# Attention masks written by ScalarE into the score bank, layer-norm spreading by transposes, and the second FFN block in another PSUM bank

## The reference

```
qkv = shift(x) @ Wqkv                    # 16 heads of 64
q, k = rotary(l2norm(q) * qs), rotary(l2norm(k) * ks)
sim  = q @ k^T * 8                       # windows of 32 queries, 64 keys (own window and the one before)
sim  = where(key > query or key < query - 32 or no such key, -max, sim)
x    = softmax(sim) @ v @ Wo + x
h    = layernorm(shift(x)) * g + b
a, gate = split(h @ W1 + b1)             # 341 + 341 columns
x    = (a * gelu(gate)) @ W2 + b2 + x
```

## Time and profile before

| | |
|---|---|
| time, median of 3 runs | 2706.54 us (2702.59 to 2709.49) |
| the profiled execution's own time | 2708.14 us |
| its span, first to last instruction | 2706.4 us |
| PE / DVE / ACT / POOL busy | 91% / 62% / 58% / 59% |
| PE weight loads busy | 62% |
| mean granted clock of TensorE | 0.964 of 2.4 GHz |
| first and last mask product (L558) | 198.6 and 2044.4 us |

### The profile page before, as it was taken

The page is one execution under the profiler, slowest core; times in us unless marked ns, Lnnn a source line. Parts: engine busy times, 40 slices in busy tenths (PEclk is TensorE's granted clock), DMA queues, the critical chain, the costliest instruction groups (busy, mean ns, idle before and its releaser), DMA issues.

```text
span 2706.4 us, 57956 instructions
## 1 busy us (share of the span) xinstructions
PE 2462.3 (91%) x23054; PEld 1687.6 (62%) x23054; DVE 1677.8 (62%) x2517; ACT 1581.8 (58%) x3162; POOL 1607.0 (59%) x931
## 2 busy tenths in 40 slices
PE   5769999999999999999999999999997888889998
PEld 3435666666666666666666666666664666656665
DVE  2347667666766666666666666766672888852222
ACT  1126666666666676667666666666662566643333
POOL 1039777777777777777777777777771322211111
PEclk8769999999999999999999999999997899989999
DMA  4002223222232222322233222322223000000000
GB/s 103 0 20 60 53 52 72 64 62 50 57 75 64 55 53 61 74 65 53 53 74 72 52 52 52 80 64 55 50 55 104 1 1 1 1 1 1 5 5 8
DMA packets 77196, 127.13 MB, mean 47 GB/s; under 512 B 24948, under 2 KB 48770, under 8 KB 76930
## 3 DMA queue, kind: packets, MB, share of 16 engines
q1 hardware_dynamic: 76930, 123.42, 19.6%
HBM read 26.56 MB, written 1.07 MB: 10 GB/s over the span
## 4 chain that ended last, share of the span: by engine, by line
PE 49%; DVE 20%; ACT 16%; issue 12%; POOL 3%; SPq 0%; DMA 0%; POOLq 0%; ACTq 0%; DVEq 0%
PE bank L601 6%; PE bank L526 6%; DVE qk L1200 6%; ACT qk L891 5%; PE bank L804 4%; PE bank L613 4%; PE bank L563 4%; PE obank L583 3%; ACT vp L903 3%; PE obank L814 2%; PE bank L814 2%; DVE n L1207 2%; PE bank L738 2%; PE lnbank L547 2%; ACT aoT L936 2%
## 5 line engine op out<-in xcount | busy, mean ns | idle before, releaser
L1200 DVE TENSOR_TENSOR qk<-bank,tab 128x1024 f32<-128x1024 f32 x384 | 470.3, 1225 | 438.2 <-ACT qk L891 438.2
L1497 POOL TENSOR_TENSOR qk<-qk 128x1024 f32<-128x1024 f32 x192 | 454.0, 2365 | 362.3 <-DVE qk L1200 362.2
L1501 POOL TENSOR_TENSOR rn<-n2m,cst 128x16 f32<-128x16 f32 x192 | 562.9, 2932 | 16.0
L526 PE MATMUL bank<-wqk,xs 128*128 128x512 f32 x768 | 400.5, 603 | 6.2 <-issue 3.7
L1505 POOL TENSOR_TENSOR qk<-qk,rn 128x1024 f32<-128x1024 f32 x192 | 365.4, 1903 | 28.1 <-POOL rn L1501 0.9
L891 ACT ACTIVATE qk<-bank 128x512 f32<-128x512 f32 x384 | 228.7, 596 | 173.2 <-PE bank L526 165.2
L537 PEld LDWEIGHTS bank<-cst,qk 128*128 128x128 f32 x1536 | 192.4, 141 | 209.8 <-issue 197.4
L1509 POOL TENSOR_TENSOR lnr<-lnv,cst 128x2 f32<-128x2 f32 (+1 forms) x88 | 66.4, 755 | 404.1 <-DVE lnv L1094 404.1
L924 ACT ACTIVATE px<-sh 128x512 f32<-128x512 f32 x192 | 121.4, 632 | 256.2 <-DVE sh L1216 255.6
L537 PE MATMUL bank<-cst,qk 128*128 128x128 f32 x1536 | 231.7, 274 | 6.6 <-POOL qk L1505 6.6
L1207 DVE TENSOR_REDUCE n<-qk 128x16 f32<-128x1024 f32 x192 | 232.2, 1209 | 0.0
(11 more groups left out here) (194 smaller groups left out, 4429.1 us busy)
## 6 DMA issues: line engine op xcount, KB each, us to landing
vp<-vp SPq DMA_DIRECT2D x672, 130.0 KB, 2.4
wqk<-in_L_ffn_Wqkv SPq DMA_DIRECT2D x24, 256.0 KB, 3.1
wv<-in_L_ffn_Wqkv SPq DMA_DIRECT2D x6, 512.0 KB, 3.6
wo<-in_L_ffn_Wo SPq DMA_DIRECT2D x6, 512.0 KB, 4.3
xs<-Z SPq DMA_DIRECT2D x48, 64.0 KB, 2.4
xs<-Z SPq DMA_DIRECT2D x48, 63.8 KB, 2.3
kT<-rel_by_distance SPq DMA_DIRECT2D x1, 2048.0 KB, 7.9
vp<-in_L_ffn_w SPq DMA_DIRECT2D x1, 2048.0 KB, 13.3
```

The lines of the kernel that those rows point to most:

```text
L526: nc.tensor.matmul(bank[s % 2][:, :], xs[:, odd, WIN + r * P:WIN + r * P + P], wqk[:, lo:lo + 512], start=True, stop=True).then_inc(p_full, 1)
L1200: tt(qk[:, both, :].rearrange("p o (h d) -> p o h d", d=DH), heads(bank[c % 2][:, :]).unsqueeze(1).broadcast_to([P, 2, PAIRS, DH]), table. ...
L1497: tt(direct, direct, swapped, ALU.add).then_inc(sum_done, 1)
L1501: tt(rn[:, m % 2, :], n2m[:, :], const("mhalf"), ALU.pow).then_inc(rn_done, 1)
```

## The change

- The mask product of L558 goes. In its place ScalarE copies the mask into `bank[3]` by a new function `seed`, placed at the end of slots 1, 3, 5 (for `scores` of slots 2, 4, 6) and 7 (for `scores` of slot 0 of the next step). It waits until `shift_scores` has read the bank (`sh_done`). `scores` now waits for `seeded`, not for `pt_done`. The first seed is still a product on TensorE, with start=True.
- `turn_probs` writes `obank[:, 0]` in place of `bank[3]`, and `take_probs` reads it there.
- `ln_wide_pe` uses a transpose in place of a product, in all four blocks.
- `hidden(f, 1)` writes `bank[4]` in place of `bank[2]`. It waits for `ot_done`, and no longer for `gate(f, 0)`. `hidden(f, 2)` waits only for `gate(f, 0)`. `turn_out` in slot 7 waits until `gate(f, 1)` has read `bank[4]`.

```diff
+HD_BANK = (2, 4, 2)
 # ln_wide_pe
-                    mm = nc.tensor.matmul(b[:, i * P:i * P + P], lnr[:, i:i + 1].broadcast_to([P, P]), ident,
-                                          start=True, stop=True)
+                    mm = nc.tensor.transpose(b[:, i * P:i * P + P], lnr[:, i:i + 1].broadcast_to([P, P]), ident)
 # scores(i, k)
-                wait(pe, pt_done, 4 * i + k)
+                pe.wait_ge(seeded, 4 * i + k + 1)
                 s = bank[3]
-                nc.tensor.matmul(s[:, :], ident_bf, maskv[:, r, :], start=True, stop=False, skip_group_check=True)
 # turn_probs(i, k)
                 pe.wait_ge(px_done, 4 * i + k + 1)
+                wait(pe, ao_done, 4 * i + k)
-                    mm = nc.tensor.transpose(bank[3][:, q * P:q * P + P], px[:, k % 2, q * P:q * P + P], ident)
+                    mm = nc.tensor.transpose(obank[:, 0, :][:, q * P:q * P + P], px[:, k % 2, q * P:q * P + P], ident)
 # turn_out(i, k)
+                if k == 3 and i >= 1:
+                    pe.wait_ge(h_done, 3 * i - 1)
 # hidden(i, c)
-                else:
-                    pe.wait_ge(h_done, 3 * i + c)
+                if c == 1:
+                    wait(pe, ot_done, 4 * i + 4 + min(3, 4 * (ITEMS - 1 - i)))
+                if c == 2:
+                    pe.wait_ge(h_done, 3 * i + 1)
...
-                    mm = nc.tensor.matmul(bank[2][0:n, half * S:half * S + S], w1[:, half * FF + c * P:half * FF + c * P + n],
+                    mm = nc.tensor.matmul(bank[HD_BANK[c]][0:n, half * S:half * S + S], w1[:, half * FF + c * P:half * FF + c * P + n],
 # before step 0
+            nc.tensor.matmul(bank[3][:, :], ident_bf, maskv[:, 0, :], start=True, stop=True).then_inc(seeded, 1)
 # ScalarE
+            def seed(i, k):
+                n = 4 * i + k + 1
+                if n < 4 * ITEMS:
+                    act.wait_ge(sh_done, n)
+                    nc.scalar.copy(bank[3][:, :], maskv[:, (n % 4) // 2, :]).then_inc(seeded, 1)
...
-                nc.scalar.copy(pT[:, k % 2, :], bank[3][:, :]).then_inc(pt_done, 1)
+                nc.scalar.copy(pT[:, k % 2, :], obank[:, 0, :]).then_inc(pt_done, 1)
 # ScalarE's step, behind take_out and ahead of exps(i, ...)
+                    if s in (1, 3, 5) and p1:
+                        seed(i, s // 2 + 1)
+                    if s == 7 and p0:
+                        seed(t, 0)
```

More of the change, by code:

```diff
@@ L245, in build @@
         mx_done, sh_done, px_done = sem("mx_done"), sem("sh_done"), sem("px_done")
+        seeded = sem("seeded")
         pt_full, pt_done = sem("pt_full"), sem("pt_done")
@@ L941, in gelu @@
                 act.wait_ge(hd_full, 3 * i + c + 1)
-                nc.scalar.activation(ge[0:n, c, :], bank[2][0:n, S:2 * S], ACT.Gelu,
+                nc.scalar.activation(ge[0:n, c, :], bank[HD_BANK[c]][0:n, S:2 * S], ACT.Gelu,
                                      bias=b1g[0:n, c, bass.ds(i // B, 1)]).then_inc(ge_done, 1)
@@ L1245, in gate @@
                 dve.wait_ge(ge_done, 3 * i + c + 1)
-                nc.vector.scalar_tensor_tensor(out=hT[0:n, c, :], in0=bank[2][0:n, 0:S], scalar=b1a[0:n, c, l],
+                nc.vector.scalar_tensor_tensor(out=hT[0:n, c, :], in0=bank[HD_BANK[c]][0:n, 0:S], scalar=b1a[0:n, c, l],
                                                in1=ge[0:n, c, :], op0=ALU.add, op1=ALU.mult).then_inc(h_done, 1)
```

## The result

The changed kernel takes 2840.89 us (median of 4 runs, 2835.82 to 2843.32) against 2707.18 us before: a ratio of 1.049, 95% interval 1.047 to 1.052. It is slower, as forecast. The size was off: 2792 was forecast, +85 us, and +134 came. That is 5 us above the end of the range, 2836.

What follows compares the result with a forecast made beforehand. The prediction took a ring of waits through TensorE, ScalarE and VectorE to bound the kernel: 2708.1 + 53 (ring) + 39 (clock falls) - 7 (outside the pipeline) = 2793, against the median 2792; range 2738 to 2836.

Steps and rivals of the forecast that it cites:

- Slots 7 and 0: `scores` starts right behind the seed, at 1054.26 and not 1054.57: 0.31 us earlier.
- Slots 1 and 2: ScalarE's unbroken run holds one seed more (0.48 us), so the squares of slot 2 are at +0.17.
- Slots 3 and 4: One seed more before the squares of slot 4; VectorE's `parts` then waits for them: +0.49 us.
- The new wait of `hidden(f, 1)` is the later one: Slot 5: waiting for `take_out` ends 0.97 us later than for `gate`; with +0.49, `hidden(f, 1)` is at +1.46.
- Slot 6: From `hidden(f, 1)` to `hidden(f, 2)` TensorE saves the mask product's 0.31 us, leaving `hidden(f, 2)` at +1.15.
- The ring: The step's loop through TensorE, ScalarE and VectorE takes 40.10 us, not 38.95: 46 x 1.15 = 53 us.
- one fall in two steps: TensorE's clock falls behind the slot 5 pause in every second step: 0.85 us per step, 39 us.
- one fall in every step: Upper end of the clock term: TensorE's clock falls behind the slot 5 pause in each step, 78 us.
- Transposes do not hold the clock: By the Trainium skill's rule, slot 5's pause begins already with `turn_out`; falls come in more than one step in two.
- the third case: Rival: the clock falls in every step, since transposes don't hold it; 2832 us, chance 0.11.
- Outside the pipeline: Spreading by transposes saves 6 us in the first block and 1 in the third and fourth: together -7.

Runs made afterwards that it cites:

- e2: The kernel before with only `hidden(f, 1)` moved to the other bank, with its new waits; masks and spreading as before: 2792.34 us (1.032).
- e1: The changed kernel with three more fp32 products of 128x512 filling the pause before `hidden(f, 1)`: 2754.72 us (1.018 of before).
- e5: The changed kernel with 24 transposes of 128x128 filling the pause before `hidden(f, 1)`: 2755.48 us (1.017 to 1.020 of before).
- e3: The changed kernel with `hidden(f, 1)` back in `bank[2]`, waiting for `gate`; seeds, probabilities' bank and transposes stay: 2727.59 us (1.008).
- e6: The kernel before with spreading by transposes and turned probabilities in the other bank; mask still a product on TensorE: 2669.89 us (0.987).

## Why the prediction was wrong in size and right in kind

Its steps, against the step of the changed kernel with the clock full:

- *Slots 7 and 0, -0.31.* `scores` starts 7.29 us behind `hidden(f, 2)` (7.30 forecast, 7.61 before in the earlier trace rows). Right.
- *Slots 1 and 2, one seed more in an unbroken run.* 5.10 us from squares to squares, forecast 4.94. Right in place; the seed is 0.52 and not 0.48, and in slot 1 it starts 0.6 behind `take_out`, not 0.48.
- *Slots 3 and 4, one seed more, and `parts` of slot 4 waits for ScalarE.* Right in place: VectorE is idle for 0.30 us there, released by the squares. They start 836.83 - 809.50 = 27.33 us behind `hidden(f, 2)`, 26.65 before: +0.68, forecast +0.49.
- *The new wait of `hidden(f, 1)` is the later one.* e2 shows it alone: 39.91 for 39.92. Right. In the changed kernel the call starts 36.12 us behind `hidden(f, 2)`, 34.47 before: +1.65, forecast +1.46. The difference of 0.19 comes from the seeds. In e2 the move, with the clock's falls, costs 2792.34 - 2705.30 = 87 us by itself, the costliest part of the change.
- *Slot 6, -0.31 for the mask product.* It is -0.23: 4.25 us for 4.48. When `scores` follows directly, the transposes take 0.53 and not 0.44.
- *The ring, 1.15 us per step.* It is 1.43; the difference is what the seeds (0.19) and slot 6 (0.08) had wrong.
- *"I take one fall in two steps ... 0.85 us per step".* **This is the step that failed.** The clock fell in 38 of 45 steps, and in 18 of them for about twice as long, which costs 2.9 us and not 1.7. Together 1.91 us per step, 86 us and not 39: 38 falls at 1.7 would be 65 us, and the longer ones add the rest. e1 confirms the sum. My share of one in two stood on two gaps; they were in another block with other work around them, and both are shorter than the pause I had forecast. The longer fall I had not considered: I took its price from one row of one length, and my "end" of one fall in every step (78 us) was no end.
- *Transposes do not hold the clock*, on which the third case rested: for fp32 transposes e5 shows the contrary. That case came nearest to the time (2832), but for another reason.
- *Outside the pipeline -7.* It is -16; the first block gained 11, my lower bound was 10.

Ring, clock and outside: forecast 53, 39, -7; measured 64, 86, -16.

What stays open: why some falls last twice as long. The trace of the changed kernel shows only where they begin. All 18 long ones begin 0.6 to 0.8 us before `hidden(f, 1)` starts, still in the pause; the 20 short ones begin at most 0.3 us before it, or up to 0.4 us behind it. Short and long ones alternate over long stretches of the 45 steps. In e2 and e3, whose pauses are shorter, every fall begins after `hidden(f, 1)` has started, and only short ones occur.

## What to carry to other kernels

Before moving work from a busy engine to an idle one, ask where the ring of waits passes. An engine's list is worked off in order, and here the 0.5 us of a seed, put into a run without a gap, moved what stood behind it by at least as much (5.10 us from squares to squares against 4.46), on an engine that had been busy for 58% of the time. A buffer freed from one wait gets another; compare the ends of both in the timeline, here 1081.38 against 1082.35. And where a pause on TensorE grows, do not price the clock from the mean of a few rows: here a pause of 2.7 us cost 1.9 us more per step behind it, which a few useless products or transposes in the pause gave back.

## What the hardware showed that I had not expected

- 24 fp32 transposes (2.8 us) in the pause were enough to keep TensorE at 2.4 GHz (e5).
- With 1.10 us of idle time at this place the clock fell in none of 45 steps (e6), with 1.71 in 8 (e3), and three useless products per step took 86 us off the changed kernel (e1).
- A copy from bf16 in SBUF to fp32 in PSUM on ScalarE takes 0.59 us for 128x512, as those from PSUM to SBUF do (0.58).
